# Fourth layer of a graph network: attention sums over 250 fixed node ranges in place of 208 edge groups

## What is computed

```python
alpha = a_src[row2] + a_dst[col2] + a_edge        # edges, then one self loop per node
alpha = jnp.where(alpha >= 0, alpha, NEG_SLOPE * alpha)
m = jax.ops.segment_max(alpha, col2, num_segments=n)
ex = jnp.exp(alpha - m[col2])
attn = ex / jax.ops.segment_sum(ex, col2, num_segments=n)[col2]
msg = attn[:, :, None] * xp[row2]
agg = jax.ops.segment_sum(msg, col2, num_segments=n)
y = (agg.reshape(n, H * OUT) + gat_bias) @ lin_W + lin_b
h = x + y                                          # layer norm (ln_g, ln_b), then
x = _layernorm(x + gat_block(...))                 # the outer residual and layer norm
```

## Time and profile before

| | us |
|---|---|
| median of 3 runs (4172.99 to 4176.88) | 4175.36 |
| the profiled execution's own time | 4196.32 |
| its span, first to last instruction | 4194.7 |
| POOL's first and last gather (start) | 2084.2, 3705.4 |
| PE's first and last matmul of the sums (start) | 3152.8, 4038.8 |
| PE's last projection (start) | 4183.0 |

### The profile page before, as it was taken

One profiled execution on the slowest core, in us unless ns is written; L12 is line 12 of the kernel. 1 busy time (PEld: TensorE's weight loads), 2 busy tenths in 40 slices (PEclk: granted clock), 3 DMA queues, 4 the chain that ended last, 5 costly groups with the idle time before them and its releaser, 6 DMA issues. The chain is left out here.

```text
span 4194.7 us, 71909 instructions
## 1 busy us (share of the span) xinstructions
PE 2500.8 (60%) x21824; PEld 2114.1 (50%) x21825; DVE 1564.4 (37%) x3762; ACT 705.3 (17%) x1093; POOL 1408.4 (34%) x1473
## 2 busy tenths in 40 slices
PE   1799998979981999699610000476602000049985
PEld 0666666858871888588500000366502000039974
DVE  4566662331136111232230000599881000025567
ACT  0378783520032000100000000000001000000023
POOL 5222121110003122143477777100006777730035
PEclk9999999979995999899855555699855555555567
DMA  3588886238844888699833333345405433335531
GB/s 110 152 274 282 270 280 201 60 120 281 281 155 127 257 251 248 198 276 281 225 106 107 101 95 101 69 95 93 85 20 144 115 111 109 105 101 151 152 91 42
DMA packets 597629, 662.88 MB, mean 158 GB/s; under 512 B 268059, under 2 KB 449388, under 8 KB 596905
## 3 DMA queue, kind: packets, MB, share of 16 engines
q1 hardware_dynamic: 276921, 405.43, 31.8%
q10 hardware_dynamic: 270440, 182.02, 16.4%
q0 software_dynamic: 50208, 74.70, 7.3%
HBM read 502.38 MB, written 159.93 MB: 158 GB/s over the span
## 5 line engine op out<-in xcount | busy, mean ns | idle before, releaser
L865 POOL DMA_INDIRECT rows<-x_rows,src_i x832 | 851.2, 1023 | 777.3 <-DVE wide L2585 497.8
L1497 PE MATMUL ps<-slices,wide 128*128 128x250 f16 x7350 | 830.8, 271 | 66.2 <-DVE wide L2163 34.3
L1497 PEld LDWEIGHTS ps<-slices,wide 128*128 128x128 f16 x7350 | 716.2, 98 | 156.8 <-DVE wide L2163 51.0
L1447 PE MATMUL ps<-weighted,slices 128*128 128x57 f32 x1664 | 367.7, 419 | 573.8 <-issue 311.6
L1723 PE MATMUL ps<-slices 128*128 128x75 bf16 x4992 | 301.0, 215 | 608.5 <-issue 516.3
L1447 PEld LDWEIGHTS ps<-weighted,slices 128*128 128x128 f32 x1664 | 358.9, 332 | 582.5 <-issue 314.3
L1723 PEld LDWEIGHTS ps<-slices 128*128 x4992 | 254.2, 107 | 655.3 <-issue 646.5
L2066 DVE TENSOR_TENSOR wide<-wide,ps 128x57 f32 x416 | 89.3, 215 | 565.0 <-remote 396.5
L905 POOL TENSOR_TENSOR ea_one<-ea,ones 128x64 f32<-128x64 f32 x250 | 131.4, 526 | 466.9 <-DMA ea<-in_edge_attr 458.9
L1392 PE MATMUL ps<-rows,weighted 128*32 128x128 f32 x2000 | 275.8, 283 | 13.4 <-DMA ea<-in_edge_attr 11.1
L2463 DVE TENSOR_TENSOR hT<-ps,hT 128x600 f32<-128x600 f32 x104 | 80.0, 779 | 536.0 <-issue 261.9
(11 more groups left out here) (354 smaller groups left out, 3424.8 us busy)
## 6 DMA issues: line engine op xcount, KB each, us to landing
slices<-adjacency SPq DMA_DIRECT2D x525, 437.5 KB, 4.4
rows<-in_edge_attr SPq DMA_DIRECT2D x250, 256.0 KB
x_of_edges<-rows SPq DMA_DIRECT2D x208, 256.0 KB
slices<-x_of_edges ACTq DMA_DIRECT2D x208, 256.0 KB
adjacency<-wide ACTq DMA_DIRECT2D x91, 437.5 KB, 3.3
adjacency<-slices ACTq DMA_DIRECT2D x84, 437.5 KB, 3.1
slices<-src_low ACTq DMA_DIRECT2D x52, 512.0 KB
rows<-x_rows,src_i POOLq DMA_INDIRECT x832
```

The source lines that it names most:

```text
L865: pool.indirect_dma_start(out=packed[i][:, c, :], out_offset=None, in_=table, in_offset=bass.IndirectOffsetOnAxis(ap=rows_of, axis=0)).the ...
L1447: mm = pe.matmul(ps_a[i][:, width * h:width * (h + 1)], rows3[i][:, n, :], weighted[:, i, n, :, :].rearrange("p h w -> p (h w)"), start=(c ...
L1497: mm = pe.matmul(ps_d[b], high_low[:, part, QS * s + q, :], slices[:, s, PN * q:PN * (q + 1)], start=(s == 0 and q == 0 and part == 0), st ...
```

## The change

The fourth layer is summed as the first is: 250 windows of 25 nodes (`LW`), each of 512 edges from `win_at`. The window's one-hot comes from `slot_of_w`, a table of the first layer that is kept. The operands of PE change places: the weights (75 columns: three heads by 25 nodes) are stationary and the rows are moving, with a column of ones added, so that 129 columns move and the last output column is the sum of the attention. DVE takes the self loop's weight as one minus that sum, multiplies the node's own row by it and adds the window's sum in one instruction (`close3`); PE turns the 75x128 result (`turn3`); DVE adds the planes of left-out edges and writes the operand of the projection (`add_left`). Every ten windows make a pair, whose projection and norms are spread over the next ten windows. `loop_weight` in DRAM, its indirect loads, the diagonals, PE's self-loop products and POOL's shifts go. ACT issues all loads: per window it reads two registers (first edge, and the count of stores that must have been made), waits for four semaphores and issues two DMAs; per pair it loads the own rows three times (25 partitions each) and once as before. POOL's stop before group 104 is kept and the one before group 112 goes. The self-loop multiplication on DVE (line 2585) goes too. Four small DVE instructions near the program's start make the table of counts. Lines with + are of the changed kernel.

```diff
-                if g == SCANNED_AT:
+                if g == NG // 2:
                     pool.wait_ge(scan_done, 1)
-                if g == SUMMED_AT:
-                    pool.wait_ge(group_summed, SUMMED + 2 * RING + 1)
                 for c in range(CH):
                     gather_chunk(i, c, src_i[:, CH * g + c:CH * g + c + 1], t3_d, rows_landed[i])
...
+            for i in range(RING):
+                pool.wait_ge(xe_stored[i], 16 * NIT)
+            missing_groups(t3_d, missing0_i)
...
-            act.dma_start(wl_d.rearrange("(p j) h -> p (j h)", p=P), XL).then_inc(scan_out, 16)
-            act.wait_ge(scan_out, 32)
...
+            act.wait_ge(scan_out, 16)
             for h in range(HEADS):
                 act.activation(wide[:, h, :], ones[:, 0:1].to_broadcast([P, NA]), ACT.Copy, scale=0.0).then_inc(scan_act, 1)
...
+            for i in range(RING):
+                act.activation(rows3[i][:, :, P:P + 1], ones[:, 0:CH].unsqueeze(2), ACT.Copy).then_inc(scan_act, 1)
+            act.wait_ge(sums_open, 1)
+            act.wait_ge(scan_act, 2 + HEADS + RING)
...
+            at_reg = act.alloc_register("act_win")
+            rounds = act.alloc_register("act_rounds")
+            def load_win(w, i):
+                if not (isinstance(w, int) and w < RING):
+                    act.wait_ge(group_summed, SUMMED + w - RING + 1)
+                act.reg_load(at_reg, win_at[0:1, bass.ds(w, 1)])
+                act.reg_load(rounds, rounds_of[0:1, bass.ds(w, 1)])
+                at = act.snap(at_reg, min_val=0, max_val=E - GE)
+                gathered = act.snap(rounds, min_val=16, max_val=16 * NIT)
+                for n in range(RING):
+                    act.wait_ge(xe_stored[n], gathered)
+                act.dma_start(rows3[i][:, :, 0:P], xe_d[bass.ds(at, GE), :].rearrange("(p c) f -> p c f", c=CH)).then_inc(rows_loaded[i], 16)
+                act.dma_start(att[:, i, :, :].rearrange("p c h -> p (c h)"), at_d[bass.ds(at, GE), :].rearrange("(p c) h -> p (c h)", c=CH)
+                              ).then_inc(att_landed[i], 16)
+            def load_own(q, s):
+                for h in range(HEADS):
+                    act.dma_start(own[LW * h:LW * (h + 1), s, :, :], t3_d[bass.ds(PN * q, PN), :].rearrange("(w n) f -> n w f", n=LW)
+                                  ).then_inc(pair_landed[s], 16)
+                act.dma_start(xb[:, s:s + 1, :, :], tiles_of(t3_d, q)).then_inc(pair_landed[s], 16)
...
+            def wins3(q, u, s, first):
+                for j in range(BW):
+                    w = BW * q + j
+                    if not (is_last(q) and j + 3 >= BW):
+                        load_win(w + 3, (BW * s + j + 3) % RING)
+                    if not is_first(q):
+                        if j == 5:
+                            root3(STEPS3 * (q - 1) + 5, 1 - s)
+                        if j == 7:
+                            root3(STEPS3 * (q - 1) + 15, 1 - s)
+                        if j == 9:
+                            store_out(q - 1, 1 - s)
+                    if j == 6 and not is_last(q):
+                        if not is_first(q):
+                            act.wait_ge(d3.step, STEPS3 * (q - 1) + 6)
+                            act.wait_ge(win_summed, BW * q)
+                        load_own(q + 1, 1 - s)
+            load_own(0, 0)
+            for w in range(3):
+                load_win(w, w)
...
+            def win3(w, v, i, b):
+                pe.wait_ge(weighted_ready, w + 1)
+                pe.wait_ge(*arrived(i, v))
+                if not few(w):
+                    pe.wait_ge(win_summed, w - 1)
+                for c in range(CH):
+                    mm = pe.matmul(ps_s[b], weighted_w[b][:, c, :], rows3[i][:, c, 0:P + 1], start=(c == 0), stop=(c == CH - 1))
+                mm.then_inc(group_summed, 1)
+            def turn3(w, b):
+                pe.wait_ge(win_summed, w + 1)
+                if not few(w):
+                    pe.wait_ge(win_copied, w - 1)
+                pe.transpose(ps_n[b], agg3[:, b, :], ident[0:WROWS, 0:WROWS]).then_inc(win_turned, 1)
+            def project(q, s):
+                pe.wait_ge(win_copied, BW * (q + 1))
+                if not early_pair(q):
+                    pe.wait_ge(d3.step, STEPS3 * (q - 2) + 1)
+                for k in range(TP):
+                    for h in range(HEADS):
+                        pe.matmul(ps_y[s][:, k, :], aT[:, s, h, TN * k:TN * (k + 1)], fused3[:, h, :], start=(h == 0), stop=False)
+                    mm = pe.matmul(ps_y[s][:, k, :], ones[0:1, 0:TN], row2[0:1, 3, :], start=False, stop=True)
+                mm.then_inc(d3.Y, 1)
+            def wins3(q, u, s, first):
+                for j in range(BW):
+                    w = BW * q + j
+                    v, i = ring_of(u, s, j)
+                    win3(w, v, i, j % 2)
+                    if not (is_first(q) and j == 0):
+                        turn3(w - 1, 1 - j % 2)
+                    if j == 2 and not is_first(q):
+                        project(q - 1, 1 - s)
...
+            v.tensor_scalar(rounds_of, ps[3][0:1, 0:NLW], float(GE - 1), None, ALU.add).then_inc(dve_step, step.up())
+            v.wait_ge(dve_step, step.n)
+            v.tensor_scalar(rounds_of, rounds_of, 11, None, ALU.arith_shift_right).then_inc(dve_step, step.up())
+            v.wait_ge(dve_step, step.n)
+            v.tensor_copy(rounds_f, rounds_of).then_inc(dve_step, step.up())
+            v.wait_ge(dve_step, step.n)
+            v.tensor_scalar(rounds_of, rounds_f, 1.0, 16.0, ALU.add, ALU.mult).then_inc(dve_step, step.up())
...
-            v.tensor_tensor(edge_by_edge(XL, HEADS), XLP, BW, ALU.mult).then_inc(scan_done, 1)
...
-            sums()
...
+            v.reciprocal(BW_, FW).then_inc(dve_step, step.up())
+            v.wait_ge(dve_step, step.n)
+            v.tensor_tensor(edge_by_edge(EX, HEADS), EXP_, BW_, ALU.mult).then_inc(scan_done, 1)
+            v.memset(not_left, 1.0).then_inc(dve_step, step.up())
+            v.wait_ge(dve_step, step.n)
+            v.wait_ge(scan_act, 2 + HEADS + RING)
+            missing_groups(missing0_i, dst_left, loaded=1, weigh=True)
+            v.memset(x_mark[:, 1:2], 0.0).then_inc(sums_open, 1)
+            def weights3(w, v_, i, b):
+                v.wait_ge(att_landed[i], 16 * (v_ + 1))
+                v.tensor_tensor(onehot_w[b], slot_of_w[:, :, bass.ds(w, 1)].to_broadcast([P, CH, LW]),
+                                iota_k[:, 0:LW, 0].unsqueeze(1).to_broadcast([P, CH, LW]), ALU.is_equal).then_inc(onehot_ready, 1)
+                v.wait_ge(onehot_ready, ONEHOTS + w + 1)
+                v.tensor_tensor(weighted_w[b].rearrange("p c (h n) -> p c h n", h=HEADS),
+                                onehot_w[b].unsqueeze(2).to_broadcast([P, CH, HEADS, LW]),
+                                att[:, i, :, :].unsqueeze(3).to_broadcast([P, CH, HEADS, LW]), ALU.mult).then_inc(weighted_ready, 1)
+            def close3(w, s, j, b):
+                v.wait_ge(group_summed, SUMMED + w + 1)
+                v.tensor_tensor(loop_w[:, b:b + 1], not_left[:, bass.ds(w, 1)], ps_s[b][:, P:P + 1], ALU.subtract).then_inc(loop_ready, 1)
+                if not few(w):
+                    v.wait_ge(win_turned, w - 1)
+                v.wait_ge(loop_ready, w + 1)
+                v.scalar_tensor_tensor(agg3[:, b, :], own[:, s, j, :], loop_w[:, b:b + 1], ps_s[b][:, 0:P], ALU.mult, ALU.add
+                                       ).then_inc(win_summed, 1)
+            def add_left(w, q, s, j, b):
+                v.wait_ge(win_turned, w + 1)
+                if j == 0 and not early_pair(q):
                     v.wait_ge(d3.Y, q - 1)
...
+                v.tensor_tensor(aT[:, s, :, LW * j:LW * (j + 1)], wide[:, :, bass.ds(LW * w, LW)],
+                                ps_n[b].rearrange("p (h n) -> p h n", h=HEADS), ALU.add).then_inc(win_copied, 1)
...
+            def wins3(q, u, s, first):
+                for j in range(BW):
+                    w = BW * q + j
+                    if j == 0:
+                        v.wait_ge(*landed3(s, u))
+                    if not (is_last(q) and j == BW - 1):
+                        v_, i = ring_of(u, s, j + 1)
+                        weights3(w + 1, v_, i, 1 - j % 2)
+                    close3(w, s, j, j % 2)
+                    if j > 0:
+                        add_left(w - 1, q, s, j - 1, (j - 1) % 2)
+                    elif not is_first(q):
+                        add_left(w - 1, q - 1, 1 - s, BW - 1, (BW - 1) % 2)
+                    if not is_first(q):
+                        if j == 4:
+                            residual3(q - 1, 1 - s)
+                        if j == 6:
+                            outer3(q - 1, 1 - s)
+                        if j == 8:
+                            normal3(q - 1, u - 1 + s, 1 - s)
+            weights3(0, 0, 0, 0)
+            pairs(v, wins3, 4)
+            add_left(NLW - 1, NP - 1, 0, BW - 1, (BW - 1) % 2)
+            residual3(NP - 1, 0)
```

(2 more changed lines are left out.)

351 lines of the change are left out of this document (93 added, 258 removed).

## The result

| | before, us | after, us | ratio, 95% interval |
|---|---|---|---|
| median of 3 runs | 4175.36 | 4383.09 | 1.050, 1.0476 to 1.0524 |
| the profiled execution's own time | 4196.32 | 4381.23 | |
| its span | 4194.7 | 4379.0 | |

The changed kernel is slower by 208 us, 5.0%. The forecast was 4312 us, 3.3% slower, with a range of 4195 to 4425: the sign and the range held. The rise is half as large again as forecast, and the result lies above the 4266 to 4370 that had been given the chance of 0.60.

What follows compares the result with a forecast made beforehand. PE held back beside the gather until 3714 us, then windows bound mainly by ACT: 3714 + 603 (232 windows at 2.6) + 14 = 4331 us of span, 4312 us as median, range 4195 to 4425.

Steps and rivals of the forecast that it cites:

- What bounds the kernel: After the scans: gather, 25 us, PE's sums, then the layer set the end; one pipeline of 250 windows replaces the last two.
- When the pipeline gets going: Second half's gather: last gather at 3689, slow PE until 3714, 18 windows done by then at 29.5 us each.
- The spell: Beside POOL's second gather: PE gets one matmul record through per 2.8 us, until 25 us after the last gather, 3714.
- The price of a window behind the gather: Window sums after 3714: 2.6 us each, mostly ACT's 2.45, for 232 windows, 603 us.
- allowance for PE's slow clock: Windows behind the gather: a little over ACT's 2.45 us, making 2.6, for stretches with PE at 1.2 GHz.
- The end: After the last load: landing, weighting, matmuls, closing, projection, norms and the store's landing, some 14 us.
- What was put at nothing: Removed POOL shifts, weight loads and diagonals, DMA packets, small DVE instructions (at most 2 us), `missing_groups`: no separate effect.
- Rival 1: Window loads slower still, through own-row transfers or ACT's register loads: 2.9 to 3.3 us a window, 4428 at 3.1; chance 0.14.
- Rival 2: Window sums: DVE is the bound, ACT's register work being cheap; 2.05 to 2.3 us a window, 4208 at 2.15; chance 0.12.
- Rival 3: Windows behind the gather cost less than 2.01 us, so the change is faster; 4161 at 1.95; chance 0.06.
- Rival 4: Second gather: PE isn't held back beside it, 199 windows done by 3689, end near 3825; chance 0.05.
- PE's clock: Window matmuls with 129 columns: some stretches at 2.4 GHz expected, halving PE's 2.3 to 2.75 us a window.

Runs made afterwards that it cites:

- e1: Changed kernel, but from window 40 on ACT neither reads the store count nor waits for stores: 3708.54 us against 3343.73 before the change, 2.42 us a window.
- e2: Changed kernel, but from pair 5 on SP issues own rows, `xb` and output stores: 3729.99 us, 2.67 us a window.
- e7: Changed kernel, but ACT reads the store count and waits for stores once in ten windows: 4279.82 us, ratio 1.0241 to the kernel before.
- e9: Changed kernel, but DVE does the own-row product and addition twice per window: 3418.27 us against 3337.17 of the kernel before, ratio 1.0242.
- e3: Changed kernel with POOL's stop before group 112 restored: 3433.21 us against 3343.73 of the kernel before, ratio 1.0258.

## Why the prediction held, and where it was off

**What bounds the kernel.** Right. The likeliest case was a pipeline bound by ACT's queue, and it is: the queue is full, three runs that took work from it (`e1`, `e2`, `e7`) quickened the windows, and one that gave DVE more (`e9`) did not slow them. That PE is held back in the job that was measured, as in the trace that the forecast was made from, is luck: in three of the five jobs it wasn't, and there the loss is 2.4 to 2.6%, as far as `e3` and `e9` stand for it.

**When the pipeline gets going.** The last gather was forecast for 3689, 3669.5 on this execution's clock, and came at 3678.4. The 13 us of POOL's stop were saved, and 3.0 of the 3.5 us of the multiplication (POOL stood for 494.8 us between the halves, against 497.8), but the rest of the second gather took 560 us against 552 (3705.4 - 3140.3 - 13.0). The spell ended 25 us behind it, as forecast, at 3703. In the earlier trace rows those 25 us were counted from POOL's last weight load at 3711.44, and the forecast put them behind the last gather, 6 us earlier; that it fits is partly chance. 18 windows were forecast by then, and 21 were closed. The first matmul came at 3152.2, where 3172 - 19.5 had put it. A window took 25.2 us, nine records of 2.8. What was off is that I spread a projection over every window (29.5 us), while the spell held only one whole projection, after the thirteenth window.

**The price of a window behind the gather.** This is the step that was too small, 2.92 us against 2.6, and it makes up the error: the windows behind the spell took 664 us in place of 603, 61 of the 67.5 us by which the span was missed (4331 - 19.5 against 4379.0). Its terms:

| ACT, us a window | forecast | measured |
|---|---|---|
| two register loads | 0.60 | 0.29 + 0.28, with gaps 0.62 |
| two DMA issues | 0.82 | 0.56 + 0.50, with gaps 1.13 |
| some nine small instructions | 0.7 | 0.65 |
| sum in the loop | 2.15 (the terms give 2.12) | 2.40 |
| a tenth of a pair's own work | 0.29 | 0.52 |
| allowance for PE's slow clock | 0.15 | none seen |
| together | 2.6 | 2.92 |

The register loads, for which the trace of before had only SP's row, were right. The term that failed is the one that had looked safe: two DMA issues at 379 ns from the earlier trace rows. The new loads have other shapes (four pieces of 512 bytes a partition in place of two of 1024, and 48 bytes in one piece in place of two of 24), and their issue took 561 and 505 ns. In the pair's share I had 0.41 us for each of five issues; the own rows' three took that, but `xb` 1.14 and the output 0.55. The span splits into 3703 + 229 x 2.90 + 12 = 4379 us: the spell's end, the last 229 windows at their mean, and what follows the last window's sum at 4367.2.

**The end.** 14 us behind the last load were forecast, and there were 18.8 (4360.2 to 4379.0).

**What was put at nothing.** No sign against it. The clearing of `wide`, which had been counted, took its 16 us.

**Rivals.** Rival 1 named this very pace, 2.9 to 3.3 us a window, with two causes. That the ring or the own rows' transfers are the limit falls by ACT's full queue, which waits for neither, and by `e1` and `e7`, which take only waits and register work away and quicken the windows; the transfers hold the ring up by 0.11 us a window once their issue is gone (`e2`). That ACT's work is longer than counted is what happened, through the DMA issues and not the register loads. Rival 2 falls by `e9`. Rival 3 needed under 2.01 us, and even with nearly half of ACT's work taken away the windows stayed at 2.29. Rival 4, PE not held back, got 0.05 on the ground that two different matmuls showed one rate. That spoke rightly against a cause in the sums, but said nothing about the job: in three of the five jobs PE wasn't held back. The time I gave for it, 3825 us (its own terms give 3689 + 51 x 2.6 + 14 = 3836 of span, 3816 on the median), missed too, since the first gather's scores and the scans then come some 500 us earlier, and since both kernels gain by it: the changed kernel's loss shrinks to 2.5%, and doesn't turn.

**PE's clock.** The granted clock was 0.73 in the steady state, with PE 63% busy, against 0.50 with PE 98% busy before. I had expected stretches at 2.4 GHz, and they are there. A window's eight records take 1.10 us in one place and 2.00 us in another, at a granted 1.00 and 0.50 (columns as in the earlier trace rows):

```profile
4000.90:4002.00 1.10, 1.10 (x10) 0.97 (x9) 0.06 (x1) 0.00 (x0) 0.00 (x0) 1.00 0.39 95
4005.40:4007.40 2.00, 2.00 (x9) 1.81 (x9) 1.74 (x9) 0.00 (x0) 0.00 (x0) 0.50 0.46 126
```

PE waited for DVE's weights at either clock (1.07 us ahead of the quick window at 4003.15, 1.11 ahead of the slow one at 4005.40), and ACT's queue was full throughout, so the clock can hardly have changed the time; it was not tried by itself. The Trainium skill (TensorE: Matmul & The Clock Gate, "Why this matters for your kernels") ties the full rate to a continuously busy TensorE; by busy time alone these two stretches stand the other way round.

## What to carry to other kernels

An engine that issues DMAs can be the bound while the profile gives it 2% busy: count the starts of its DMA issues per iteration, and compare their spacing with the sum of its instructions. When a load changes its shape, take the issue's length as unknown; here it was 1.3 to 1.5 times the nearest row. Moving DMAs to another queue frees the issuing engine, but their transfers still delay the others. Time a change against the old kernel in the same job each time, since the same program took 3340 us in one job and 4178 in another, and the loss differed by half.

## What the runs showed of the hardware

- In two jobs PE, and SP beside it, went slowly while POOL gathered with indirect DMAs, and in three they did not, with the same gathers at the same pace (304 and 305 POOL instructions in 400 us). PE got 153 matmul records through in 400 us in one case and 4951 in the other; a move on SP took 692 ns and 29 ns at the median. The kernel before took 4175 to 4178 us and 3337 to 3360 us at the median. The cause was not found.
- In the slow spell the records of a window's eight matmuls stand together within 2 us, and their result is taken 17 us later. The group of the earlier trace rows had the same count of records by time, so the rate by count was right, but the place of a single record says little there.
- ACT's DMA issues took 561 ns for 128x4x128 and 505 for 128x12, against 379 for both 128x2x256 and 128x2x6 before, and 1140 for 125x2x128 (`xb`) behind three others. Fewer pieces did not make it shorter. Another difference is that the window loads take their address from a register that was read from a table; SP's window loads of the first layer do too, and took 333 ns (lines 632 and 636 of the kernel before). What sets the length was not tried.
- Writing ACT's loop out removed two small register instructions ahead of each register load (35 and 51 ns, some 0.15 us with their gaps) and gave 24 us of 4280, as ACT then waited itself for some of it.
